# Two attention and mixture-of-experts layers on one core: the routing groups cut at 10 and 6 batches in place of 8 and 8

## What is computed

```python
x = x + attn_a(layernorm(x), wq, wk, wv)      # one head, rotated q and k, softmax
x = x + ffn(layernorm(x), W1, b1, W2, b2, Wr, br)
x = x + attn_b(layernorm(x), w_q, w_k, w_v, w_o)   # 16 heads of 64, causal
x = x + ffn(layernorm(x), W1, b1, W2, b2, Wr, br)

def ffn(x, ...):                  # 8 experts, each token goes to one
    logits = x @ Wr + br
    idx = argmax(logits); gate = softmax(logits)[idx]
    for ei in range(8):
        h = gelu(x @ W1[ei] + b1[ei])          # 128 -> 512
        y = h @ W2[ei] + b2[ei]                # 512 -> 128
        out += y * (gate where idx == ei)
```

## Time and profile before

| | |
|---|---|
| median of 3 runs | 983.93 us (983.05 to 984.64) |
| the profiled execution's own time | 987.06 us |
| its span, first to last instruction | 984.9 us |
| mean granted TensorE clock | 0.934 |
| busy share | PE 86%, VectorE 66%, ScalarE 57%, GpSimd 45% |

### The profile page before, as it was taken

The page is one execution under the profiler, slowest core; times in us unless marked ns, Lnnn a source line. Parts: engine busy times, 40 slices in busy tenths (PEclk is TensorE's granted clock), DMA queues, the critical chain, the costliest instruction groups (busy, mean ns, idle before and its releaser), DMA issues. The chain is left out here.

```text
span 984.9 us, 24722 instructions
## 1 busy us (share of the span) xinstructions
PE 843.6 (86%) x6756; PEld 706.2 (72%) x6756; DVE 645.8 (66%) x2713; ACT 557.7 (57%) x2089; POOL 441.0 (45%) x755
## 2 busy tenths in 40 slices
PE   5888665399979999999999979989999999538993
PEld 4676555399967778777877857867877787538993
DVE  4888866166647776776767687667667666615665
ACT  2444343166657766776676656666667666315661
POOL 3333362555534444443434424674444444074552
PEclk9999777599979999999999999999999999768996
DMA  9900012302010000000000000001000000021214
GB/s 335 320 14 0 9 36 78 105 32 78 32 52 2 1 2 2 2 2 2 1 2 1 0 1 2 18 29 62 0 1 0 0 2 1 4 99 41 78 35 144
DMA packets 25936, 40.05 MB, mean 41 GB/s; under 512 B 4656, under 2 KB 17584, under 8 KB 24816
## 3 DMA queue, kind: packets, MB, share of 16 engines
q1 hardware_dynamic: 20848, 28.76, 9.0%
q0 software_dynamic: 4992, 10.27, 3.2%
HBM read 20.58 MB, written 18.43 MB: 40 GB/s over the span
## 5 line engine op out<-in xcount | busy, mean ns | idle before, releaser
L378 POOL TENSOR_SCALAR pb<-pb,rib 128x128 f32<-128x128 f32 x256 | 96.0, 375 | 307.1 <-DVE rib L789 306.0
L804 DVE CUSTOM_DVE_ANT_0 PS<-PS,CST 128x128 f32<-128x128 f32 (+1 forms) x512 | 167.8, 389 | 62.0 <-PE PS L1022 49.6
L473 ACT ACTIVATE yT<-PS,w1b 128x128 f32<-128x128 f32 x368 | 105.3, 369 | 115.7 <-remote 48.1
L503 ACT COPY qk<-PS 128x512 f32<-128x512 f32 x128 | 75.1, 587 | 155.6 <-PE PS L880 155.6
L334 POOL DMA_INDIRECT yt_dram<-XY x92 | 97.8, 1063 | 82.0 <-DVE XY L737 78.4
L840 DVE COPY pT<-PS 128x384 f32<-128x384 f32 x256 | 130.6, 551 | 1.8 <-PE PS L1033 1.1
L1022 PE MATMUL PS<-qk 64*128 64x128 f32 (+1 forms) x1024 | 120.0, 353 | 8.2 <-ACT pb L520 6.6
L520 ACT ACTIVATE pb<-PS,nbb 128x256 f32<-128x256 f32 x256 | 125.3, 490 | 0.0
L380 POOL TENSOR_SCALAR pb<-pb,rib 128x256 f32<-128x256 f32 x256 | 123.2, 481 | 0.0
L1001 PE MATMUL PS<-yT 128*128 128x128 f32 x736 | 102.9, 285 | 20.8 <-ACT yT L473 12.8
L1033 PE MATMUL PS<-CST,pb 128*128 128x128 f32 x768 | 110.8, 277 | 10.8 <-POOL pb L380 9.9
(11 more groups left out here) (129 smaller groups left out, 1769.8 us busy)
## 6 DMA issues: line engine op xcount, KB each, us to landing
xs_dram<-XY SPq DMA_DIRECT2D x4, 1483.5 KB, 13.4
XY<-xs_dram SPq DMA_DIRECT2D x4, 1225.5 KB, 6.1
W1S<-in_W SPq DMA_DIRECT2D x1, 2048.0 KB, 20.9
W2S<-in_W SPq DMA_DIRECT2D x4, 512.0 KB, 7.7
out_dram<-X SPq DMA_DIRECT2D x8, 256.0 KB, 4.4
yt_dram<-XY POOLq DMA_INDIRECT x92
XY<-xs_dram SPq DMA_DIRECT2D x4, 258.0 KB, 2.7
xs_dram<-TOK,POS POOLq DMA_INDIRECT x64
```

Source lines behind the costliest of these rows:

```text
L473: last = nc.scalar.activation(hT[:, v, c, :], PS[:, v, c * P:(c + 1) * P], ACT.Gelu, bias=w1b1[:, v, F + c:F + c + 1])
L804: last = nc.vector.tensor_tensor_reduce(ps, ps, CST[:, m:m + c1 - c0], -SCALE_B, HIGHEST, ALU.add, ALU.min, nbb[:, hh % 4, c0 // P:c0 // P ...
```

## The change

The groups are of 10 and 6 batches. A layer still has 46 expert tiles, now 27 and 19; there are still 32 scatters in a layer, now 20 and 12. `route(0)` and its scatters move from step 14 to step 16, and the scatters go at 4 a step. `route(2)` moves behind two more batches of attention B; its 20 scatters go behind the 16 heads of batch step 13. The first loop of `expert_steps` now runs to step 23. The last group is gathered in 3 pieces. The zero fills, loads, tables and slices take each group's own size, and one buffer (`qks`) moves out of `XY`. The diff, cut to its core:

```diff
-GB = NB // GROUPS
-GT = GB * TPB
-NJ = GT + E - 1
-NL = GROUPS * NJ
+GBS = (10, 6)
+GB0 = (0, GBS[0])
+GTS = tuple(n * TPB for n in GBS)
+GT0 = (0, GTS[0])
+NJS = tuple(n + E - 1 for n in GTS)
+NJ0 = (0, NJS[0])
+GT, NJ = max(GTS), max(NJS)
+NL = sum(NJS)
...
-LENT = 20
-XCHUNKS = ((0, 4), (4, NJ))
+LENT = NL - 3 - NJS[0]
+XCHUNKS = ((0, 4), (4, None))
...
-    second, tail = NJ // RING * RING, NL // RING * RING
+    second, tail = NJS[0] // RING * RING, NL // RING * RING
...
-        qks = lent[:, 4 * TPB * M:4 * TPB * M + 2 * M]
+        qks = pT.rearrange("p a b -> p (a b)")[:, 0:2 * M]
...
-                sp.wait_ge(scattered[k], 16 * GT)
+                sp.wait_ge(scattered[k], 16 * GTS[g])
...
-                        for q in range(4) if kk == 3 else (0,):
+                        for q in range(gt // 4) if kk == 3 else (0,):
...
             turns(pool, attn_a, 8, 14)
             for s in range(14, NB + 5):
                 attn_a(s, s % 2)
-                if s == 14:
+                if s == 16:
                     before_scatters(0)
-                for t in range(3 * (s - 14), min(3 * (s - 13), GT)):
+                for t in range(4 * (s - 16), min(4 * (s - 15), GTS[0])) if s >= 16 else ():
                     scatter(0, t)
             before_scatters(1)
-            for t in range(GT):
+            for t in range(GTS[1]):
                 scatter(1, t)
...
                 if h == 0:
                     before_scatters(2)
-                scatter(2, h)
+                for t in range(GTS[0] * h // H, GTS[0] * (h + 1) // H):
+                    scatter(2, t)
...
-            turns(pool, attn_b, 4, 10)
-            attn_b(10, 0)
-            attn_b(11, 1, scatter2)
-            turns(pool, attn_b, 12, 16)
+            turns(pool, attn_b, 4, 12)
+            attn_b(12, 0)
+            attn_b(13, 1, scatter2)
+            turns(pool, attn_b, 14, 16)
             peeled(attn_b, 16, 18)
             before_scatters(3)
-            for t in range(GT):
+            for t in range(GTS[1]):
                 scatter(3, t)
...
             peeled(attn_a, 0, 8)
-            turns(dve, attn_a, 8, 14)
+            turns(dve, attn_a, 8, 16)
             route(0)
-            turns(dve, attn_a, 14, 16)
```

More of the change, by code:

```diff
@@ L45 @@
 C_SCAN = C_E8 + E
-C_TILE = C_SCAN + E * GT
+C_TILE = C_SCAN + E * sum(GTS)
 C_W = C_TILE + NJ * E
@@ L119, in sem @@
             return ctx.enter_context(nc.semaphore(name))
-        xs_dram = [nc.dram_tensor(f"xs_dram{k}", [P * NJ, DI], F32, kind="Internal").ap() for k in range(4)]
+        xs_dram = [nc.dram_tensor(f"xs_dram{k}", [P * NJS[k % GROUPS], DI], F32, kind="Internal").ap() for k in range(4)]
         yt_dram = [nc.dram_tensor(f"yt_dram{k}", [NONE + P * NJ, D], F32, kind="Internal").ap() for k in range(4)]
@@ L316, in scatter @@
             def scatter(k, t):
-                tile = GT * (k % GROUPS) + t
+                tile = GT0[k % GROUPS] + t
                 nc.gpsimd.indirect_dma_start(
@@ L323, in before_scatters @@
                 pool.wait_ge(r_step, STEPS * (k + 1))
-                pool.wait_ge(r_tok, GB * (k + 1))
+                pool.wait_ge(r_tok, batches(k))
                 pool.wait_ge(s_xs0, 64)
             def give_back(k):
-                for j in range(NJ):
+                for j in range(NJS[k % GROUPS]):
                     if k == 1 and j == LENT:
                         attn_b(0, 0)
-                    tile = NJ * (k % GROUPS) + j
-                    pool.wait_ge(f_y, NJ * k + j + 1)
+                    tile = NJ0[k % GROUPS] + j
+                    pool.wait_ge(f_y, NL * (k // GROUPS) + tile + 1)
                     nc.gpsimd.indirect_dma_start(
@@ L667, in over_e @@
                 def over_e(ap):
[L668 to L672, removed]
[L673 removed]
+                    return ap.unsqueeze(2).to_broadcast([P, gt, E])
+                dve.wait_ge(r_lg, batches(k))
@@ new lines, in route @@
+                    in1=e_t(exc), op0=ALU.mult, op1=ALU.add))
+                then(nc.vector.tensor_tensor(e_t(exc), pre, e_t(exc), ALU.add))
+                then(nc.vector.tensor_tensor(e_t(exc), e_t(exc), e_t(hot), ALU.mult))
+                then(nc.vector.reduce_sum(pos, e_t(exc).rearrange("p e t -> p t e"), AX.X))
+                then(nc.vector.tensor_copy(posi, pos))
+                then(nc.vector.tensor_scalar(rtile, posi, 7, None, ALU.logical_shift_right))
+                then(nc.vector.tensor_copy(tilef, rtile))
@@ L714, in route @@
+                then(nc.vector.tensor_scalar(pos, pos, float(nj), None, ALU.mult))
+                then(nc.vector.scalar_tensor_tensor(out=POS[:, t0:t0 + gt], in0=tilef,
+                                                    scalar=float(1 - nj * P), in1=pos, op0=ALU.mult,
                                                     op1=ALU.add))
                 then(nc.vector.tensor_tensor(
-                    r_cmp[:, :, :], CST[:, C_TILE:C_TILE + NJ * E].rearrange("p (j e) -> p j e", e=E),
-                    r_cum[:, None, :].to_broadcast([P, NJ, E]), ALU.is_ge))
@@ L753, in step @@
                             for c, (j0, _) in enumerate(XCHUNKS):
-                                if fixed(j) and j == (kk * NJ if kk else j0):
+                                if fixed(j) and j == (NJ0[kk] if kk else j0):
                                     dve.wait_ge(xs_in[GROUPS * layer + kk][c], 16)
@@ L808, in attn_b @@
                     if p == 1 and has(s):
-                        if fixed(s) and s in (0, GB):
-                            dve.wait_ge(gathered[s // GB], 16)
+                        if fixed(s) and s in GB0:
+                            dve.wait_ge(gathered[GB0.index(s)], 16)
                         combine(TPB * s, b_comb)
```

128 lines of the change are left out of this document (67 added, 61 removed).

## The result

| | before | after |
|---|---|---|
| median, 5 runs each | 984.0 us (983.05 to 985.1) | 989.4 us (988.22 to 990.66) |
| ratio | | 1.0051 (1.0037 to 1.0066) |
| the profiled execution, its span | 987.06, 984.9 us | 988.28, 986.4 us |
| mean granted clock | 0.934 | 0.93 |

What follows compares the result with a forecast made beforehand. PE was taken as full in attention B and most expert tiles, with stalls entering the expert tiles that keep GpSimd's scatter and load timetable. Terms 0.2 + 4.6 + 0.5 + 4.0 - 6.3 - 0.8 = +2.2 us gave 986.1 us, range 977 to 997.

Steps and rivals of the forecast that it cites:

- the sum: All terms over the whole kernel added up: +2.2 us, 986.1 us on the median, own range 983 to 989, chance 0.55.
- Start, +0.2: At the kernel's start, larger constants on the first transfer, 560 KB in place of 480, cost 0.2 us.
- Layer 0, the first scatters, +10.9: Before layer 0's experts, 20 scatters start later and end 10.9 us later, delaying the load that route(1) waits for.
- Layer 0, the second scatters, -0.5 - 5.1 - 0.7: Up to layer 0's restart, narrower route(1), four fewer scatters and a smaller load give back, leaving +4.6 us.
- Attention B, +0.5 and +4.0: In attention B, a longer route(2) costs 0.5 us and four more group 2 scatters in one batch 4.0.
- Layer 1, -6.3: Up to layer 1's restart, narrower route, fewer scatters and smaller load save 6.3 us; nothing pushes route(3) later.
- The end, -0.8: At the kernel's end, the last gather in 3 pieces in place of 4 saves 0.8 us.
- Stalls that shrink by more than the scatters: Rival at the expert tiles' start: 5.2 us more gained in each layer, -8.2 us, 975.7 us; chance 0.18.
- Hidden first scatters: Rival in layer 0: the first scatters' 10.9 us partly hidden, layer 0 comes out even, -2.4, 981.5 us; chance 0.07.
- A fixed stall at the loop's entry: Rival at the first expert loop: stall length unchanged whatever the scatters, +13.8 us, 997.7 us; chance 0.15.

Runs made afterwards that it cites:

- b_pT: The kernel before with only the buffer qks moved from XY into pT: 940.6 us, 1.0042, on the chip where before took 936.7 us.
- a_lateload: The changed kernel with the second group's load held back until 14 expert tiles of the layer are done: 987.83 us, 1.0034 to before.
- before_again: The kernel before, unchanged, run again for a second trace and the noise: 985.16 us, 1.0005, traced span 981.5 us.
- l0_only: The kernel before with groups of 10 and 6 in layer 0 only, layer 1 at 8 and 8, qks in pT: 993.61 us, 1.0089.
- l1_only: The kernel before with groups of 10 and 6 in layer 1 only, layer 0 at 8 and 8, qks in pT: 984.37 us, 0.9997.
- b_unroll: The kernel before with the first loop of the expert steps written out in all engines: 984.94 us, 0.9991.
- b_late: The kernel before with the second group's scatters in both layers begun only when 12 expert tiles are done: 1014.14 us, 1.0291.
- a_vb: The changed kernel with qks in vb in place of pT: 950.05 us, 1.0141 to before, on the chip where before took 936.7 us.

## Why the prediction came out as it did

The forecast was 986.1 us and slower as the likeliest sign; it is 989.4. That is inside the whole range of 977 to 997, just outside the 983 to 989 that the sum's own terms were given, and 3.3 us above the number; of the 5.4 us measured the sum had 2.2. So the direction was right and over half of the cost was missed. The ledger shows where each term went.

*Start, +0.2.* Attention A's first residual sum comes at 28.59 us, where the two traces of before have 27.85 and 28.18 and the other eleven 28.2 to 29.4. That is too wide to read 0.2 us from.

*Layer 0, the first scatters, +10.9.* The mechanism was right: they end at 157.51 + 0.96 = 158.5 us (156.1 forecast), the load goes out at 159.81, and the copy inside the route comes at 162.61 (160.2 forecast) after a wait of 9.27 us (9 forecast). All of it is 2.4 us late, because attention A is. `route(1)` begins 4.6 us later, not 2.2. The step that failed is a term that the sum left at nothing without a reason: `qks` moved out of `XY`. `b_pT` gives it 3.9 us (2.1 to 5.9). The start of `route(1)` over all 14 traces parts the two: it lies at 146.1 to 149.5 us (mean 147.8) in the five with `qks` in `XY`, at 150.4 in the two that only moved the buffer in layer 0, and at 152.0 to 153.0 (mean 152.5) in the seven that also have layer 0 at 10 and 6. That is some 2.6 us for the buffer and 2.1 for the later scatters, where the sum had 2.2 for the scatters.

*Layer 0, the second scatters, -0.5 - 5.1 - 0.7.* From first scatter to restart it is 29.73 us before and 24.20 after, 5.5 us less, where 5.8 (the scatters and the load) were forecast. The size was nearly right and a part of the reason wrong: the load has nothing in it (`a_lateload`), so its 0.7 us, and the load as a sign to go by, came true by luck. By the reading above it is the unbroken run of indirect DMAs that counts, scatters and give backs, and 21 of them became 16 here.

*Attention B, +0.5 and +4.0.* The stage cost 3.7 us (10.4 - 6.8), 0.8 less than the two terms. `route(2)`'s batch takes 42.1 us where 41.5 stood, so +0.5 was right. The other term was too large. The earlier trace rows show one batch, but only 9 of the 16 scatters fall in it, and after the change 12 of 20; the others are in the batch ahead. The two batches together take 34.1 + 38.2 us before and 34.7 + 39.6 after, some 2 us more, and the batch that I said would take about 42 us takes 39.6. From first to last scatter it is 4.0 us longer (39.3 for 35.3), so half of it is caught up again. I took GpSimd to have no slack. The earlier trace rows already had 4.2 + 0.9 us of its waits for `rib`. The rest of the 3.7 us, about 1, is spread over other batches.

*Layer 1, -6.3.* From the start of `route(3)` to the restart it is 44.65 us before and 38.21 after, -6.4. The size is right; the load's share in it is not, as in layer 0.

*The end, -0.8.* From the restart to the end of the span it is 95.4 us before and 92.9 after, -2.5. Against `before_again` (95.2) it is -2.3. The sign was right and the size too small. From the first of the last gathers (971.44 and 974.78 us) to the end it is 13.4 and 11.6 us, -1.8, and that is the part that the term was for; the other 0.6 us lies ahead of the gathers. No experiment took this apart.

*The sum* was +2.2 on a trace; trace against trace it is +1.5, median against median +5.4. The two don't contradict: the trace of before lies 3.1 us above its median, and that of after lies 1.1 us below its own. Against `before_again` the traces differ by +4.9. What I missed is then some 3 us, and the buffer's 2.4 to 3.9 us would account for them; the errors of the other terms, of 1 to 2 us each, go both ways.

*The rivals.* Stalls that shrink by more than the scatters: no, 24.2 us in both layers. Hidden first scatters: no, 9.27 us of wait. A fixed stall at the loop's entry: refuted where the stall exists, by the length that goes with the count (`l0_only`, `l1_only`), by the loop written out (`b_unroll`), and by the loop entered at full speed (`b_late`). It was argued with a rule of the Trainium skill ("Runtime: NRT & Kernel Launch", Instruction fetch mechanics), by which a branch to a page not held has to wait for its fetch. The section calls this a DMA fetch and says nothing of what sets its length, so "a stall that no count of scatters sets" was my reading of it. The trace does not bear the rule out here. The DMA view of `before_again` from 157 to 192 us, in which gelu waits 14.39 and 7.22 us, lists two queues only:

```profile
q1 hardware_dynamic: 288, 1.52, 12.4%
q0 software_dynamic: 640, 1.32, 11.4%
```

The page of the profile has 96 packets of instructions for the whole span, and none falls in this window. In `b_late` none falls between 172.5 and 229 us, and the stall lies from 187 to 226. One can fall into a stall: in the trace of before one does at about 190.7 us, 2 us ahead of the restart, and in `b_unroll` one at about 185.7, 9 us ahead of it; the stalls are as long with such a packet as without.

Where there is no stall, one half of this rival holds: what can't shrink gives nothing back. On the third chip `a_vb` costs 13.3 us, close to the rival's +13.8, but that is luck, since the rival too had no price for the buffer. Against `b_pT`, which has a slow place as well, `a_vb` costs 9.5 us. Stage by stage, `a_vb` against `b_pT` there and after against before here: from `route(1)` to the first residual sum of attention B it is +6.0 and +2.2 us, from `route(3)` to the first of the last gathers -1.7 and -7.1. Fewer second scatters are worth what they save of a stall, and where there is none they save little.

*Open.* The runs don't show by what path a run of indirect DMAs delays what PE hands to ScalarE and VectorE, nor why one chip of three is free of it. Each chip had one set of runs, so it isn't shown either that the chip is the cause, and not something else that differed between the sets. That a gap between the transfers would end the stall was not tried. The traces only suggest it: in attention B, where two scalings stand between most scatters, PE is busy 34.5 of 39.6 us.

## What to carry to other kernels

A stall that keeps another engine's timetable should be tied to it by moving that timetable: a distance that repeated to 0.1 us in two layers of one trace varied by 1.5 us in the next and was half wrong about its cause, and one kernel with the work shifted by 12 tiles said more than all the arithmetic on it. Where a split of work shortens one half and lengthens the other, count where each half is exposed: here layer 1's late half was worth having, layer 0's early half was not, and the two can be chosen apart. Every line of a diff wants a price, a buffer's new address too. And a number that comes true is no proof of its rival: 13.3 met 13.8 with a 4 us term missing from it.

## What the runs showed of the hardware that was not expected

- The same kernel took 985 us on two chips and 936.7 on a third. Some 47 of the 48 us are in the stages of the two stalls: from `route(1)` to the first residual sum of attention B 178.1 us (`before_again`) against 155.1 (`b_pT`), from `route(3)` to the first of the last gathers 126.6 (before) against 102.2 (`b_pT`). Each chip was used for one set of runs.
- With 16 to 31 indirect DMAs in an unbroken run on GpSimd, 1.26 us apart, ScalarE and VectorE could take results of PE only late on two of three chips: a gelu up to 21.9 us after its product's end with the scatters in their usual place (`before_again`), and 34.6 us in `b_late`. PE's update of the semaphore was itself recorded that late (226.42 us in `b_late`). In the other direction PE took a copy of VectorE's 0.06 us after its end.
- A GpSimd product of two 128x512 operands took 1.11 us with its input in one place of SBUF and 1.27 or 1.28 us in two others.
- In layer 0 of `b_late`, the granted clock fell from 1.00 to 0.50 while the engines stood.
